# Routing one batch of a mixture of experts inside the attention ahead of it, on one core of Trainium2

## What is computed

```python
def _dispatch(xb, pb, cap):
    top_k_probs, ei = jax.lax.top_k(pb, K)
    flat = ei.swapaxes(0, 1).ravel()
    one_hot = jax.nn.one_hot(flat, E, dtype=jnp.int32)
    pos = jnp.cumsum(one_hot, axis=0) * one_hot
    ...
    buf = buf.at[ei2.ravel(), pos.ravel()].set(xr, mode='drop')
...
gate_probs = jax.nn.softmax(g, axis=-1)
...
h = jax.nn.silu(gg) * h
o = jnp.einsum('enh,ehc->enc', h, w_proj)
...
y = jax.vmap(_collect)(expert_outputs, indices, positions, top_k_probs)
```

## Time and profile before

| what | us |
| --- | --- |
| median of 3 runs (2140.4 to 2143.22) | 2142.18 |
| the profiled execution's own time | 2142.47 |
| its span, first to last instruction | 2140.7 |
| TensorE busy | 1966.8 |
| VectorE busy | 1748.2 |
| ScalarE busy | 1512.3 |
| GpSimd busy | 44.3 |
| mean granted TensorE clock | 0.969 of full |

### The profile page before, as it was taken

How to read it: one execution, slowest core, us unless ns; L and a number is a source line. 1 busy time by engine, 2 the same in 40 slices (tenths; PEclk the granted TensorE clock), 3 DMA queues, 4 the chain that set the end, 5 groups by cost and what they waited for, 6 DMA issues and landing times.

```text
span 2140.7 us, 30896 instructions
## 1 busy us (share of the span) xinstructions
PE 1966.8 (92%) x11354; PEld 794.9 (37%) x11354; DVE 1748.2 (82%) x1657; ACT 1512.3 (71%) x1918; POOL 44.3 (2%) x58
## 2 busy tenths in 40 slices
PE   7799999999999998999999999999888999985493
PEld 3233333333333333333333333333224444443382
DVE  5589999999999998799999999999975676665244
ACT  2388888888888886688888888888843555552020
POOL 2000000000000000000000000000000000000203
PEclk9899999999999999999999999999999999998697
DMA  5533323333233332133323333223300000021884
GB/s 189 190 104 94 90 79 89 89 94 94 75 89 91 92 101 87 50 90 89 94 75 94 90 89 99 75 84 77 131 21 1 1 1 1 1 89 32 283 280 143
DMA packets 112586, 194.55 MB, mean 91 GB/s; under 512 B 10288, under 2 KB 63536, under 8 KB 112432
## 3 DMA queue, kind: packets, MB, share of 16 engines
q1 hardware_dynamic: 109872, 184.12, 29.2%
q0 software_dynamic: 2560, 8.39, 1.2%
HBM read 108.58 MB, written 50.33 MB: 74 GB/s over the span
## 4 chain that ended last, share of the span: by engine, by line
PE 80%; DVE 8%; issue 4%; DMA 4%; ACT 2%; POOL 1%; SPq 1%; POOLq 0%; ACTq 0%; DVEq 0%
PE ps L964 21%; PE ps L1082 20%; PE ps L882 11%; PE ps L879 11%; PE ps L989 5%; PE ps L1145 3%; DVE dacc L1483 2%; PE ps L1017 2%; PE ps L952 1%; PE ps L1155 1%; DMA kscr<-wsm 1%; PE ps L995 1%; PE ps L1045 1%; PE ps L1030 1%; DMA kst<-kscr 1%
## 5 line engine op out<-in xcount | busy, mean ns | idle before, releaser
L1319 ACT ACTIVATE pt<-ps,bias 128x1024 f32<-128x1024 f32 x1024 | 1109.4, 1114 | 222.5 <-PE ps L1082 221.3
L1483 DVE TENSOR_TENSOR dacc<-dacc,pt 128x2048 f32<-128x2048 f32 x504 | 1152.9, 2288 | 49.0 <-ACT pt L1319 22.9
L1082 PE MATMUL ps<-qst,kst 128*128 128x512 f16 x2048 | 615.1, 383 | 19.8 <-ACT pt L1319 19.0
L964 PE MATMUL ps<-pt,vt 128*32 128x512 f32 x4096 | 495.4, 601 | 0.0
L1082 PEld LDWEIGHTS ps<-qst,kst 128*128 128x128 f16 x2048 | 178.3, 98 | 423.9 <-ACT pt L1319 131.3
L879 PE MATMUL ps<-wsm 128*128 128x512 f16 x1152 | 315.0, 384 | 14.8 <-DVE wsm L1440 10.8
L882 PE MATMUL ps<-wsm 128*128 128x512 f16 x1152 | 310.8, 380 | 5.5 <-ACT vt L1200 2.9
L964 PEld LDWEIGHTS ps<-pt,vt 128*32 128x32 f32 x4096 | 107.1, 109 | 263.6 <-issue 243.1
L879 PEld LDWEIGHTS ps<-wsm 128*128 128x128 f16 x1152 | 113.5, 99 | 157.8 <-issue 10.8
L882 PEld LDWEIGHTS ps<-wsm 128*128 128x128 f16 x1152 | 112.4, 98 | 145.2 <-issue 4.2
L1284 ACT ACTIVATE pr<-ps,nmx 128x128 f32<-128x128 f32 (+3 forms) x128 | 66.4, 523 | 117.0 <-DVE nmx L1585 116.7
(11 more groups left out here) (186 smaller groups left out, 1250.6 us busy)
## 6 DMA issues: line engine op xcount, KB each, us to landing
kscr<-wsm SPq DMA_DIRECT2D x128, 256.0 KB, 3.5
kst<-kscr SPq DMA_DIRECT2D x128, 256.0 KB, 3.4
kst<-kst SPq DMA_DIRECT2D x128, 256.0 KB, 3.4
wsm<-in_ctx SPq DMA_DIRECT2D x32, 768.0 KB, 4.7
qst<-qscr SPq DMA_DIRECT2D x32, 128.0 KB, 2.9
xbuf<-xn SPq DMA_DIRECT2D x16, 256.0 KB, 6.6
wsm<-in_gate SPq DMA_DIRECT2D x8, 512.0 KB, 5.0
wsm<-in_fc SPq DMA_DIRECT2D x8, 512.0 KB, 5.9
```

The lines of the kernel that those rows point to most:

```text
L964: p = e.matmul(ps[32 * h:32 * h + 32, 4 + n % 2, :], vt[:, kb % 2, ch, c:c + 32], pt[:, (2 * i + h // 2) % 6, h % 2, :], start=ch == 0, st ...
L1082: p = e.matmul(ps[:, 2 * half + h2, :], kst[:, kb % 2, h, ch * 128:ch * 128 + 128], qst[:, h, :], start=True, stop=True)
L1319: e.activation(pt[:, (2 * i + half) % 6], ps[:, 2 * half:2 * half + 2, :], ACT.Exp, bias=bias[:, 4 * kb + ch:4 * kb + ch + 1], scale=SCORE ...
L1483: e.tensor_tensor(own_heads, own_heads, probs, ALU.add).then_inc(S["add"], 1)
```

## The change

The routing is cut in two, one half for each batch of four tiles. The tiles of numbers it uses move out of the feed-forward stage's memory, so that they exist during the attention. The first batch's half becomes eight events in the list: `rank`, `odds`, `shares`, `first`, `second` in slots 6, 8, 9, 11, 13 of tile 5, `cum` in slot 4, `place` in slot 5 and `rows` in slot 7 of tile 6. `cum` uses columns 128 to 255 of bank 1, and `p4` of tile 7 now waits for `place`. The second batch's half stands behind the list. GpSimd issues eight scatters after each half. Operations are also merged: product and sum in one (scalar_tensor_tensor), the one-hot rows written in bf16 at once, the row of the scatter as a maximum, the conversion to whole numbers done by the last operation. SP's program is unchanged.

```diff
@@ self_order
         if 1 <= a < 8:
             for step in (carry if a < 7 else late).get(k, ()):
                 follow(a - 1, step)
+        if a == 6 and k == 4:
+            out.append(("cum", 0, 1, fill((1,))))
...
+        if a == 5 and k in (6, 8, 9, 11, 13):
+            out.append((("rank", "odds", "shares", "first", "second")[(6, 8, 9, 11, 13).index(k)], 0))
+        if a == 6 and k == 5:
+            out.append(("place", 0, 1))
+            empty((1,), "cumr", 1)
+        if a == 6 and k == 7:
+            out.append(("rows", 0))
...
+    for what in ("rank", "odds", "shares", "first", "second"):
+        out.append((what, 1))
+    out.append(("cum", 1, 5, ()))
+    out.append(("place", 1, 5))
+    out.append(("rows", 1))
@@ pool
-            e.wait_ge(S["dst"], 1)
             e.wait_ge(S["zero"], 256)
-            for j in range(16):
...
+            for b in range(2):
+                e.wait_ge(S["dst"], b + 1)
+                for k in range(2):
+                    for t in range(4 * b, 4 * b + 4):
+                        e.indirect_dma_start(out=xbuf, out_offset=bass.IndirectOffsetOnAxis(ap=diu[:, k, t:t + 1], axis=0),
+                                             in_=xn3[:, t, :], in_offset=None).then_inc(S["sct0"], 16)
+            e.wait_ge(S["ciu"], 2)
@@ pe
+                elif what == "cum":
+                    b, bank_ = t, ev[2]
+                    e.wait_ge(S["ohb"], b + 1)
+                    for x in range(8):
+                        for q in range(x + 1):
+                            p = e.matmul(ps[:, bank_, 128 + 16 * x:144 + 16 * x], (trib if q == x else onesb)[:],
+                                         ohb[:, q // 4, 4 * b + q % 4], start=q == 0, stop=q == x)
+                    p.then_inc(S["cum"], 1)
@@ act
+                elif what == "odds":
+                    e.wait_ge(S["lgs"], t + 1)
+                    e.activation(pp[:, 4 * t:4 * t + 4], lg[:, 4 * t:4 * t + 4], ACT.Exp).then_inc(S["pexp"], 1)
@@ dve
+                elif what == "rank":
...
+                elif what == "shares":
...
+                elif what in ("first", "second"):
...
+                    e.tensor_reduce(tp[:, k, tiles], pp[:, tiles], AX.X, ALU.max).then_inc(S["dve"], 1)
...
+                    e.scalar_tensor_tensor(out=w3[:, tiles], in0=w3[:, tiles], scalar=-100.0, in1=i100, op0=ALU.mult,
+                                           op1=ALU.add).then_inc(S["dve"], 1)
...
+                        e.tensor_tensor(ohb[:, 1, tiles], wide(ei[:, 1, tiles]), i0, ALU.is_equal).then_inc(S["ohb"], 1)
...
+                elif what == "place":
+                    counts = ps[:, ev[2], 128:256].rearrange("p (k t n) -> p k t n", k=2, n=16)
+                    e.wait_ge(S["cum"], t + 1)
+                    e.tensor_tensor(w3[:].rearrange("p (k t) n -> p k t n", k=2), counts, ohb[:, :, 4 * t:4 * t + 4, :],
+                                    ALU.mult).then_inc(S["cumr"], 1)
+                elif what == "rows":
...
+                    e.scalar_tensor_tensor(out=dr[:, :, tiles], in0=po[:, :, tiles], scalar=64.5, in1=tro[:, :, tiles],
+                                           op0=ALU.is_ge, op1=ALU.mult).then_inc(S["dve"], 1)
...
+                    e.tensor_tensor(diu[:, :, tiles], ci[:, :, tiles], dr[:, :, tiles], ALU.max).then_inc(S["dst"], 1)
+                    e.tensor_copy(ciu[:, :, tiles], ci[:, :, tiles]).then_inc(S["ciu"], 1)
```

More of the change, by code:

```diff
@@ L555 @@
  e0 e1 e2 e3 e4 e5 e6
- lgs pexp ohb cum dst sct0 xl0 xl1 xl2 xl3 eT xeT up sgx hT dn oe os0 os1 y out
+ lgs pexp ohb cum cumr dst ciu sct0 xl0 xl1 xl2 xl3 eT xeT up sgx hT dn oe os0 os1 y out
 """.split()
@@ L633, in build @@
         lg = sb("lg", [128, 8, 16], F32)
+        pp = sb("pp", [128, 8, 16], F32)
+        w3 = sb("w3", [128, 8, 16], F32)
+        ohb = sb("ohb", [128, 2, 8, 16], BF16)
+        v8 = sb("v8", [128, 8], F32)
+        tp = sb("tp", [128, 2, 8], F32)
+        ei = sb("ei", [128, 2, 8], F32)
+        po = sb("po", [128, 2, 8], F32)
+        ci = sb("ci", [128, 2, 8], F32)
+        dr = sb("dr", [128, 2, 8], F32)
+        ciu = sb("ciu", [128, 2, 8], U32)
+        diu = sb("diu", [128, 2, 8], U32)
         s3 = ExitStack()
@@ L831, in pool @@
                    allow_small_or_imprecise_dtypes=True)
-            e.iota(tro[:], pattern=[[128, 16]], base=2048, channel_multiplier=1, allow_small_or_imprecise_dtypes=True)
-            e.iota(bof[:].rearrange("p (k b t) -> p k b t", k=2, b=2), pattern=[[0, 2], [64, 2], [0, 4]], base=0,
-                   channel_multiplier=0, allow_small_or_imprecise_dtypes=True)
+            e.iota(tro[:].rearrange("p k t -> p (k t)"), pattern=[[128, 16]], base=2048, channel_multiplier=1, allow_small_or_imprecise_dtypes=True)
             e.affine_select(out=maskm[:], in_=maskm[:], compare_op=ALU.is_ge, fill=1e30, base=0,
@@ L969, in self_piece @@
                 what, t = ev[0], ev[1]
-                if what in ("turn", "p01", "p23", "p4", "qkT", "wo", "rT", "router", "score"):
+                if what in ("turn", "p01", "p23", "p4", "qkT", "wo", "rT", "router", "score", "cum"):
                     for name, value in ev[-1]:
@@ L1116, in pe @@
                 self_piece(ev)
[L1118 to L1125, removed]
             def e_turn(x):
@@ L1660, in dve @@
                 self_piece(ev)
[L1662 to L1699, removed]
-                    e.tensor_tensor(w3[:, 4 * b:4 * b + 4], cum, oh[:, k, 4 * b:4 * b + 4],
-                                    ALU.mult).then_inc(S["dve"], 1)
-                    e.wait_ge(S["dve"], own.up())
-                e.tensor_reduce(po[:, k, :], w3[:], AX.X, ALU.add).then_inc(S["dve"], 1)
-                e.wait_ge(S["dve"], own.up())
@@ L1705, in dve @@
-            f = "p k t -> p (k t)"
-            e.tensor_scalar(dr[:], po[:], 64.5, None, ALU.is_ge).then_inc(S["dve"], 1)
-            e.wait_ge(S["dve"], own.up())
-            e.tensor_scalar(po[:], po[:], 64.0, -1.0, ALU.min, ALU.add).then_inc(S["dve"], 1)
-            e.wait_ge(S["dve"], own.up())
-            e.scalar_tensor_tensor(out=ci[:].rearrange(f), in0=ei[:].rearrange(f), scalar=128.0, in1=po[:].rearrange(f),
-                                   op0=ALU.mult, op1=ALU.add).then_inc(S["dve"], 1)
@@ L1712, in dve @@
-            e.wait_ge(S["dve"], own.up())
-            e.tensor_tensor(ci[:].rearrange(f), ci[:].rearrange(f), bof[:], ALU.add).then_inc(S["dve"], 1)
-            e.wait_ge(S["dve"], own.up())
-            e.tensor_copy(ciu[:], ci[:].rearrange(f))
-            e.tensor_tensor(di[:].rearrange(f), tro[:], ci[:].rearrange(f), ALU.subtract).then_inc(S["dve"], 1)
-            e.wait_ge(S["dve"], own.up())
-            e.tensor_tensor(di[:], di[:], dr[:], ALU.mult).then_inc(S["dve"], 1)
-            e.wait_ge(S["dve"], own.up())
@@ L1720, in dve @@
-            e.tensor_tensor(di[:], di[:], ci[:], ALU.add).then_inc(S["dve"], 1)
-            e.wait_ge(S["dve"], own.up())
-            e.tensor_copy(diu[:], di[:].rearrange(f)).then_inc(S["dst"], 1)
             for x in range(16):
```

66 lines of the change are left out of this document (46 added, 20 removed).

## The result

The changed kernel took 2128.99 us (median of 4 runs, 2127.39 to 2129.6) against 2141.37 (4 runs, 2140.4 to 2143.22): ratio 0.9935, 95% interval 0.9923 to 0.9947. Timed again beside other runs it gave 0.9941 (0.9927 to 0.9954). The profiled execution took 2129.05, span 2127.3.

What follows compares the result with a forecast made beforehand. The serial chain behind the last logits (routing, sixteen scatters, landing, expert inputs load) was taken as the bound. Gain there -11.8 plus attention cost 2.8 gave -9.0 us: 2133.2 us, range 2130.2 to 2138.6.

Steps and rivals of the forecast that it cites:

- Eight scatters and the shorter routing: Behind the last logits: eight fewer scatters save 10.3 us, shorter routing 4.0; 14.2 us if nothing else comes last.
- What comes last next: Before the expert stage: bytes queued ahead of the first quarter of expert inputs limit the gain to 11.8 us.
- rival B: Before the expert inputs: scatters lose to the weights, landing as these drain; gain 9.9, time 2135.1 us; chance 0.12.
- a dip to 200 GB/s ahead of the load: Transfer rate before the expert inputs load: a dip near 200 would mean scatters, not bytes, were last.
- The moved half: First batch's routing inside attention tiles 5 and 6: costs 2.8 us, bounds 0.8 and 7.3.
- lower bound of 0.8: Routing moved into the attention: at least 0.8 us of added time, only what cannot be hidden.
- Untouched stages: Stretches before the first score minimum and from the first expert transpose to the end: 0 us change.
- The early scatters: First batch's eight scatters beside the attention, from about 1897 us on: cost nothing.
- rival E: Tile 6: GpSimd's scatters hold VectorE off for 10.3 us; attention grows 17.6, time 2148.0 us; chance 0.04.
- A: Before the expert stage: DMA limit does not bind, inputs load once issued; gain 14.2, time 2130.8 us; chance 0.12.
- C: Attention absorbs none of the moved routing, paying all 7.3 us; time 2137.7 us; chance 0.16.
- D: All sixteen scatters still stand behind the attention; only 4.0 us shorter routing against 2.8; time 2141.0 us; chance 0.03.

Runs made afterwards that it cites:

- fewer_ops: The kernel before with the merged operations alone, both batches' routing still behind the attention; 2141.18 us against 2142.13, ratio 0.9993.
- after_again: The changed kernel profiled a second time with no edit; 357.0 us from first score minimum to last logits.

## Why the prediction missed, point by point

**Eight scatters and the shorter routing.** Right: scatters in steps of 1.27 us for 1.28, the last index ready 7.2 us behind the start of the logits copy, where I had 7.5 (1973.7 to 1981.2) and the kernel before 11.5.

**What comes last next.** The size was right (11.5 for 11.8), the mechanism wrong. I had the bytes ahead of the first quarter as the limit. It was rival B's mechanism: the scatters, among the weights, landed late (6.2 us for 2.7) and the load began only then. My sign for it, a dip to 200 GB/s ahead of the load, is the 173 above. Its price was 11.5 and not 9.9, since the last scatter landed at 1993.1, 22.5 us behind the logits and 1.4 sooner on that scale than the drained weights of my sum (1997.6 less 1973.7). Both orders with fewer weights ahead show it.

**The moved half.** This is where the forecast of the time failed. Place by place I had 2.8 us (the places add up to 2.7) with bounds of 0.8 and 7.3. At full clock it is 1.9 with the scatters: 0.9 in tile 5 where I had 1.1 (first, shares and second), 1.0 in tile 6 where I had 1.6. This is a term of the sum, too big by 0.9. But the step that failed is another: I took TensorE's clock in the attention as given. From the first score minimum to the last logits the profile of the changed kernel has 0.4 us *less* than that of before, as TensorE had the lower clock for less of the time behind minimum 54 (64.6 us for 66.7). With the scatters elsewhere this repeats: five profiles have 64.4 to 64.6 there and 353.2 to 354.0 in all, five without routing in the attention 66.7 to 66.9 and 354.0 to 354.7. With the scatters in tile 6 it is in part luck: the other three profiles of the changed kernel have 357.0 to 361.1. My lower bound of 0.8, "only what cannot be hidden", could not be one. Of the 4.4 us between -9.0 and -13.4, 3.2 are here.

**Untouched stages.** -2.7 and +1.2 where I had nothing. The first is spread between executions, shown by twenty profiles; it is luck, and the changed kernel's profile had the good end of it. The second may lie in part behind the restart: TensorE ran its first experts longer at the low clock. I had read the earlier trace rows (0.53 in the first 3.6 us, then full) as the same for both; from 2002.2 to 2005.6 the changed kernel still had 0.85 (the profile of fewer_ops, without the moved half, had 0.80 there, counted from its first transpose):

```profile
1998.60:2002.20 3.60, 3.59 (x16) 3.36 (x17) 0.00 (x0) 1.20 (x2) 0.00 (x0) 0.50 1.02 393
2002.20:2005.60 3.40, 3.40 (x28) 3.40 (x27) 0.00 (x0) 0.00 (x0) 0.00 (x0) 0.85 1.05 391
```

My range was made of the terms' bounds alone. Runs of the unaltered kernel before spread over 7 us (2138.19 to 2145.39); a range for a single median of three or four needed one or two more at either end, and 1.2 were missing. All eleven executions of the changed kernel lie between 2127.1 and 2137.8, seven of them below the range, four inside.

**The early scatters.** I had them at no cost, and this is wrong, though the first profile hides it. The stall is 1.9 to 2.1 us, in eight of ten. It isn't rival E as I described it, VectorE held by the common ports for all eight: ScalarE too goes on late, and both waited for TensorE. What holds it up is open; it needs the scatters in tile 6, and it comes without weights and with half idle DMA engines as well. Profiles with it have 356.9 to 361.1 us of attention, those with no scatter beside the attention 353.2 to 354.7 and those with the scatters in tile 7 353.4 to 354.0. That is 2 to 8 us more, of which 2 are the stall and the rest a lower clock. Whether the stall brings that clock isn't shown: after_again has 357.0 us without a stall. The kernel with scatters in tile 7 pays neither. Why some executions of the changed kernel escape isn't shown.

**Rivals A, C, D** didn't come about: the last scatter's landing held the load back, the attention absorbed 5.4 of 7.3 us at full clock, and the early scatters were early.

## What to carry to other kernels

When a serial chain is shortened beside a queue of transfers, write down both limits, bytes and landings, and also ask what the backlog does to the landing of the small transfers in it; here an undisturbed landing (2.7 us) became 6. Put bulk loads that are needed later behind the load that the next stage waits for. A range must hold more than the terms of the edit: profile the unaltered kernel more than once, and cut the profiles at landmarks that both kernels have, since two whole spans mix the edit with the clock and with stages that it never touched.

## What the runs showed of the hardware

VectorE and GpSimd do lengthen each other's instructions. The changed kernel, VectorE and GpSimd beside each other as the first scatter runs, and later:

```profile
1896.95 0.30 DVE L1396 TENSOR_SCALAR mt<-mt 128x32 f32<-128x32 f32 x1
...
1899.19 0.79 DVE L1607 TENSOR_SCALAR pr<-pr,rsi 128x384 f32<-128x384 f32 x2
1899.89 1.21 DVE L1579 TENSOR_TENSOR qc<-qc,amp 128x1024 f32<-128x1024 f32 x1
...
1902.35 1.21 DVE L1579 TENSOR_TENSOR qc<-qc,amp 128x1024 f32<-128x1024 f32 x1
```

```profile
1896.08 1.20 POOL L862 DMA_INDIRECT xbuf<-xn,diu  x1 [1866.06 <-DVE diu L1686]
...
1900.12 1.82 POOL L862 DMA_INDIRECT xbuf<-xn,diu  x1 [0.30 <-issue]
1902.24 0.96 POOL L862 DMA_INDIRECT xbuf<-xn,diu  x1 [0.30 <-issue]
```

With all scatters late the first two VectorE rows take 0.18 and 0.75:

```profile
1898.39 0.18 DVE L1396 TENSOR_SCALAR mt<-mt 128x32 f32<-128x32 f32 x1
...
1900.50 0.75 DVE L1607 TENSOR_SCALAR pr<-pr,rsi 128x384 f32<-128x384 f32 x2
```

The first ends here at 1897.25, where the scatter ends (1897.28), and the stretch from minimum 52 to 53 takes 5.84 us for 5.68; the operations with two inputs keep their durations. GpSimd pays more: 1.82 for 0.96 where the scatter starts 0.23 us behind a multiplication of two tiles. By the Trainium skill, SBUF — State Buffer, SBUF: two separate sides, a VectorE operation in a two-port mode, or one with two inputs in SBUF against a GpSimd one that reads SBUF, and a GpSimd operation exclude each other for a whole instruction. The trace agrees only in part: the multiplication at 1902.35 starts 0.11 us into a scatter and neither is longer than alone, and the pair at 1899.19 grows by 0.04 us beside a scatter of 0.96. The price to VectorE was 0.16 us for eight scatters. My sentence that no stretched operation bears this out held for the end of the kernel only.

The stall beside indirect scatters, 1.9 to 2.1 us in which ScalarE and VectorE wait for TensorE, is the other, and its cause is open. And a landing depends on what else is queued: the last of the same eight scatters lands 2.7 us after its issue behind 3.1 MB of weights and 5.9 to 6.2 behind 6.3 MB.
